# Six stages of attention and expert networks on one core: attention's steps in another order, the sort's one-hot blocks eight at a time, and every semaphore opened at the program's start

## What is computed

```python
x = x + 0.5 * _L0_ffn_ref(_layernorm(x), ...)      # stage 0
x = x + _L0_attn_ref(_layernorm(x), ...)           # stage 1
x = x + 0.5 * _L0_ffn_ref(_layernorm(x), ...)      # stage 2
x = x + 0.5 * _L1_ffn_ref(_layernorm(x), ...)      # stage 3
x = x + _L1_attn_ref(_layernorm(x), ...)           # stage 4
x = x + 0.5 * _L1_ffn_ref(_layernorm(x), ...)      # stage 5

# _L0_attn_ref: patches of 20 tokens at a stride of 2
dots = jnp.einsum('brhsd,brhtd->brhst', q, k) * scale
out = jnp.einsum('brhst,brhtd->brhsd', jax.nn.softmax(dots, axis=-1), v)

# _L1_attn_ref: causal, with a table by clipped distance
scores = (scores + jnp.einsum('bhqd,qkd->bhqk', Qh, rel_k)) / scale
attn = jax.nn.softmax(jnp.where(causal[None, None], scores, -1e9), axis=-1)
out = jnp.einsum('bhqk,bhkd->bhqd', attn, Vh) + jnp.einsum('bhqk,qkd->bhqd', attn, rel_v)

# _L1_ffn_ref: two of eight experts for each token, and a shared one
top_v, top_i = jax.lax.top_k(probs, K)
out_e = jnp.einsum('etf,efd->etd', silu(flat @ w1_e) * (flat @ w3_e), w2_e)
routed = jnp.einsum('te,etd->td', gates, out_e)
return alpha * shared + (1.0 - alpha) * routed
```

## Time and profile before

| | before |
|---|---|
| median of three runs | 1068.61 us (1068.46 to 1072.13) |
| the profiled execution's own time | 1070.65 us |
| span of the profiled execution | 1068.9 us |
| PE busy | 872.8 us (82%) |
| DVE busy | 691.8 us (65%) |
| ACT busy | 458.4 us (43%) |
| POOL busy | 307.1 us (29%) |
| mean granted clock of PE | 0.916 of full speed |

### The profile page before, as it was taken

One profiled execution on the slowest core, in us unless ns is written; L12 is line 12 of the kernel. 1 busy time (PEld: TensorE's weight loads), 2 busy tenths in 40 slices (PEclk: granted clock), 3 DMA queues, 4 the chain that ended last, 5 costly groups with the idle time before them and its releaser, 6 DMA issues.

```text
span 1068.9 us, 21934 instructions
## 1 busy us (share of the span) xinstructions
PE 872.8 (82%) x7943; PEld 684.8 (64%) x7943; DVE 691.8 (65%) x2146; ACT 458.4 (43%) x807; POOL 307.1 (29%) x391
## 2 busy tenths in 40 slices
PE   2899946777769999699999936788887768999996
PEld 1788824444558788588888813445444447988885
DVE  5586556879785877674444458788888558444444
ACT  1333304576744336324554401545455533345542
POOL 5572001001405246205666301000000010266641
PEclk9999965999988999799999956989899868999998
DMA  8800000000000001001111020000000010011113
GB/s 235 260 2 1 1 1 1 2 2 2 2 2 1 2 2 31 11 1 38 42 45 40 16 79 1 2 1 2 2 2 1 2 40 1 15 47 42 46 27 121
DMA packets 27734, 31.26 MB, mean 29 GB/s; under 512 B 5999, under 2 KB 20214, under 8 KB 27632
## 3 DMA queue, kind: packets, MB, share of 16 engines
q1 hardware_dynamic: 22640, 20.55, 6.4%
q0 software_dynamic: 4992, 9.32, 3.3%
HBM read 22.51 MB, written 8.26 MB: 29 GB/s over the span
## 4 chain that ended last, share of the span: by engine, by line
PE 58%; DVE 27%; ACT 9%; issue 3%; DMA 1%; POOL 1%; DVEq 0%; SPq 0%; POOLq 0%; ACTq 0%
PE bank L1397 9%; PE banks0to L1359 5%; PE banks0to L814 5%; DVE score_max L1615 5%; PE banks0to L1360 5%; PE banks0to L1361 5%; PE bank L1383 4%; PE banks0to L822 4%; PE bank L833 3%; PE bank L1886 3%; ACT stacks_and_choice L1798 2%; PE banks0to L1866 2%; DVE expert_sum L563 2%; PE banks0to L1871 2%; ACT hidden L1793 2%
## 5 line engine op out<-in xcount | busy, mean ns | idle before, releaser
L1078 DVE TENSOR_TENSOR hidden<-silu_gate,banks0to 128x512 f32<-128x512 f32 x110 | 75.6, 688 | 146.0 <-PE banks0to L1361 144.5
L1811 ACT ACTIVATE normed_T<-banks0to 128x1024 f32<-128x1024 f32 x80 | 82.5, 1032 | 103.4 <-PE banks0to L1871 103.2
L1291 ACT COPY hidden<-bank 128x512 f32<-128x512 f32 x110 | 64.5, 586 | 132.2 <-PE bank L1383 132.2
L1397 PE MATMUL bank<-l_w,hidden 128*128 (+1 forms) x880 | 117.8, 277 | 2.7 <-ACT hidden L1291 2.7
L1397 PEld LDWEIGHTS bank<-l_w,hidden 128*128 128x128 f32 x880 | 110.2, 193 | 13.3 <-ACT hidden L1291 3.7
L1615 DVE TENSOR_REDUCE score_max<-banks0to 128x8 f32<-128x1024 f32 x80 | 97.6, 1220 | 19.8 <-PE banks0to L1871 17.5
L1256 POOL DMA_INDIRECT stacks_and_choice<-l_ffn_normed,v_tokens x78 | 75.6, 970 | 117.9 <-DVE v_tokens L1243 94.0
L1268 POOL DMA_INDIRECT l_ffn_results<-normed_T,v_tokens x78 | 78.3, 1004 | 73.8 <-DVE normed_T L1099 42.9
L563 DVE SCALAR_TENSOR_TENSOR expert_sum<-bank,gate,expert_sum 128x128 f32<-128x128 f32 x224 | 63.0, 343 | 48.8 <-PE bank L833 47.1
L197 POOL TENSOR_TENSOR ln_rstd<-ln_var_eps,minus_half 128x4 f32<-128x4 f32 x24 | 25.4, 1060 | 236.4 <-DVE ln_var_eps L190 236.4
L1285 ACT ACTIVATE silu_gate<-banks0to 128x512 f32<-128x512 f32 x110 | 65.8, 598 | 44.9 <-PE banks0to L1361 42.9
(11 more groups left out here) (281 smaller groups left out, 1906.0 us busy)
## 6 DMA issues: line engine op xcount, KB each, us to landing
l_w<-in_L_ffn_w_e SPq DMA_DIRECT2D x2, 2048.0 KB, 13.5
stacks_and_choice<-l_ffn_results SPq DMA_DIRECT2D x8, 512.0 KB, 5.6
l_w<-in_L_ffn_w SPq DMA_DIRECT2D x1, 2048.0 KB, 10.1
l_ffn_normed<-stacks_and_choice SPq DMA_DIRECT2D x7, 256.0 KB, 2.3
stacks_and_choice<-l_ffn_normed,v_tokens POOLq DMA_INDIRECT x78, 2.6
l_ffn_results<-normed_T,v_tokens POOLq DMA_INDIRECT x78, 2.3
x_tokens<-in_L_attn_x SPq DMA_DIRECT2D x4, 256.0 KB, 3.7
out_x<-x_tokens SPq DMA_DIRECT2D x4, 256.0 KB, 2.3
```

The source lines that it names most:

```text
L1078: v.tensor_tensor(net.hidden[:, i % 2, :], net.sil[:, i % 2, :], net.bank[2 + i % 2], ALU.mult).then_inc(self.gated.sem, 1)
L1397: ins = mm(net.bank[5 + i % 2][:, 0:D], net.hiddenT[:, i % 2, f, :], w2, start=(f == 0), stop=(f == FT - 1))
L1811: nc.scalar.activation(net.pT[:, i % 2, :, :], net.scores[:, 1], ACT.Exp).then_inc(self.exps.sem, 1)
```

## The change

Nothing that is computed changes, and no instruction goes to another engine. All increments of `prime` move to the start of the program, on each engine. In attention the division of tile 1 moves up to stand right behind that of tile 0; q_stack and k_stack are signalled after each query tile; the first sequence's second projection goes to banks 6 and 7, so that it need not wait until DVE has read banks 4 and 5; and the statistics of groups 1 and 2 stand in front of the reading of the first projection, with group 3 in front of the first maxima. In stage 4 the statistics of group 0 and the first normalisation are done among the last adds of stage 3. In TokenChoice the three operations on one-hot blocks become four times three over eight choices each, one set behind each `at_rows`, and the product of unit 3 moves in front of them; `count` moves on PE behind the next `up`.

```diff
     def token_choice(...):
-        every = [P, T * TOP, BLOCKS]
-        chain.then_wait(v.tensor_tensor(net.which_block, ... .to_broadcast(every), flat(net.choice_block), ALU.is_equal))
-        unit(3)
-        v.tensor_tensor(net.in_block[:, :, 0, :], net.which_block, flat(net.choice_number), ALU.mult)
-        v.tensor_tensor(net.in_block[:, :, 1, :], net.which_block, flat(net.choice_gate),
+        unit(3)
+
+    def in_blocks(self, dve, chain, r):
+        at, every = slice(r * RING, (r + 1) * RING), [P, RING, BLOCKS]
+        chain.then_wait(v.tensor_tensor(net.which_block[:, at, :], ... .to_broadcast(every), flat(net.choice_block), ALU.is_equal))
+        v.tensor_tensor(net.in_block[:, at, 0, :], net.which_block[:, at, :], flat(net.choice_number), ALU.mult)
+        v.tensor_tensor(net.in_block[:, at, 1, :], net.which_block[:, at, :], flat(net.choice_gate),
                         ALU.mult).then_inc(self.placed.sem, 1)
         for r in range(T * TOP // RING):
             at_rows(r)
+            self.in_blocks(dve, chain, r)
...
             step(late + 4 + r)
         def move(c):
-            if c == 0:
-                pe.wait_ge(self.placed.sem, self.placed.at(0, 1))
             if c % RING == 0:
+                pe.wait_ge(self.placed.sem, self.placed.at(0, c // RING + 1))
...
                 up(i + 1)
+            if i == self.late + 1:
+                count()
...
                 turn_hidden(i)
-            if i == self.late:
-                count()
...
         for g in range(groups):
...
+            if attention and g == 1:
+                dve.wait_ge(*self.group_done(0))
+                attention.spread.vector(dve, 0)
+            if attention and g == 2:
+                attention.spread.wait(dve, 0)
+                attention.normalise(dve, 0)
...
 class Attention:
+    def projected(self, n, tt):
+        banks = self.net.bank
+        return banks[6:8] if n == 0 and tt == 1 else banks[4:6]
...
         def split(...):
-            ins.then_inc(self.stacks.sem, 1)
+                ins.then_inc(self.stacks.sem, 1)
         def first():
-            normalise(0)
+            if not self.begun:
+                self.normalise(dve, 0)
...
+            for g in range(1, 3):
+                self.spread.vector(dve, g)
             for tt in range(TPB):
                 project(0, 0, tt, front)
             split(0, 0, front)
...
-            for g in range(1, T // GROUP):
-                self.spread.vector(dve, g)
-            self.spread.wait(dve, T // GROUP - 1)
+            self.spread.vector(dve, T // GROUP - 1)
             project_and_maximise(0, 0)
...
                 finish(n, 0, back)
...
+                finish(n, 1, back)
             project_and_maximise(n + 1, 1 - b, with_max, with_front, then, late)
             if with_max:
                 values(n + 1, 1 - b)
-            finish(n, 1, back)
...
         def stacks(n, b, groups):
             for g in groups:
+                if g % 2 == 0:
+                    pe.wait_ge(self.stacks.sem, self.stacks.at(n, g // 2 + 1))
                 if g == 0:
-                    pe.wait_ge(self.stacks.sem, self.stacks.at(n, 1))
...
         def _(dve):
             for stage in made:
+                stage.prime_vector(dve)
+            for stage in made:
```

127 lines of the change are left out of this document (75 added, 52 removed).

## The result

The changed kernel takes 1061.11 us (median of 11 runs, 1054.1 to 1063.8); the kernel before, beside it, 1068.82 us (11 runs). The ratio is 0.9908 with a 95% interval of 0.9888 to 0.9928: faster by 0.7 to 1.1%. The time lies inside the predicted range (1049.5 to 1063), but the gain is 7.7 us where 12.5 were forecast. The eleven runs lie in two groups, five at 1054.1 to 1058.6 us with a mean granted clock of 0.928 to 0.932 and six at 1061.1 to 1063.8 with 0.915 to 0.918; the profile is of one of the six (1063.62 us), so what it says of lost clock is shown for those alone.

A forecast was written before the change was run, and what follows sets the result against it. PE was busy 82% and DVE 65%, with the bound changing from stage to stage. The terms summed to 12.5 us off the profiled 1070.65, 1058.1; that execution stood 2.0 over the median, so 1056, range 1049.5 to 1063.

The forecast's parts named there:

- The start: Start of the program: DVE's 35 semaphore openings, now all first, delay the first statistic; a loss of 0.4 us.
- the six turns: First attention's turns: early division gains 0.2 us in each of six, the last turn loses; taken as 0 in all.
- The first TokenChoice's start and sort: First TokenChoice up to its first move: start +1.7, count +0.6, shorter block operations; first move 5.2 us sooner.
- The rounds: Three later rounds of each sort, which take over nine block operations: a loss of 0.1 us each.
- The second attention's lead: Second attention up to PE's first stacks: earlier statistics, free banks and half signals gain 6.3 us (4.5 to 6.5).
- The second sort and the clock behind it: Second TokenChoice: the same sort gain, +2.6 us, and +3.4 us from PE's clock no longer halved behind the first move.
- the term of -7.0: Second attention's turns: early division waits 1.2 us for `by_token`, losing 1.0 us seven times; ends -11 and 0.
- the slower rival: PE's clock falls in each turn of both attentions, 2.0 us a turn, giving 1081 us; chance 0.04.
- this rival (gains taken back by row transfers): Gains ahead of TokenChoice's units are taken back by the row fetches, about 1066 us; chance 0.03.
- that the clock held at the second sort: Second TokenChoice's first move: shorter PE wait keeps full clock, +3.4 us; rival that it falls, 1059.5 us, chance 0.15.
- a loss in the first attention's turns: Rival: first attention's `by_token` isn't ready either, so seven turns lose 1.0 us each, 1063 us; chance 0.08.

The follow-up runs named there:

- The taken-back versions: One-hot blocks whole on the changed kernel: 1068.19 us; openings at each stage's head, 1046.36, and count before the `up`, 1049.05, on the kernel with late division and two fillers.
- the runs with one and with three waits filled: Changed kernel plus unread PE transposes in second-attention turns: 16 before the shifted queries, 1060.83 us; also 8 and 14 at two mid-turn waits, 1055.54 us.
- the kernel with the late division and two fillers: Changed kernel with second attention's tile 1 division behind the next maximum again, plus 8 and 14 unread transposes at two mid-turn PE waits: 1046.77 us, ratio to before 0.9800.
- the kernel with three fillers: Changed kernel plus 16, 8 and 14 unread transposes at three PE waits of each second-attention turn: 1055.54 us.

## Why the prediction was right, and where it was short

**Right by its steps.** The start lost 0.4 us (first statistic at 4.14). Up to stage 2's first add 2.3 us were gained (356.17 to 353.89), the forecast for the start and the first attention together: 2.7 by the second sequence's first maximum with the start's loss in it (183.67 to 181.00; 2.3 forecast), 0.4 in each of six turns at full clock (17.4 to 17.0; 0.2 forecast), and the last turn's loss, foreseen at 1.0, of 1.1. The reason given for the six turns was not right: their second divisions wait for nothing without the earlier stacks too. The first TokenChoice's start and sort gave 5.5 for 5.2. The taken-back versions, against the changed kernel's stretch, give 2.9 for the blocks (2.85), 2.0 for the openings (1.7) and 0.6 for the count (0.6), the last two with the clock at half in more of the stretch. The rounds cost 0.12 us each (4.63 in place of 4.51). The second attention's lead gave 6.3 for 6.3. The second sort and the clock behind it gave 5.8 for 6.0.

**The step that costs was named, and its size was not.** The early division waits for `by_token` (1.16 us [<-PE], 1.2 forecast), and a turn without loss of clock is 0.9 us longer (25.9 against 25.0), 1.0 forecast. Mis-sized is the term of -7.0: its price went by turns at full clock, and there it was right, 6.7 us from the stage's first maximum to its end (219.2 against 212.4). In the profile that stretch lost 9.5 us (218.6 to 228.1), within the term's own lower end of -11, and taking the step back alone gave 11.7 in the medians. The difference is clock: the changed kernel's profile lies 9.0 us above the 219.2, the profile before 6.2 above the 212.4. I had it as the slower rival, at 0.04 and against the 2.12 us of wait at 469.70 that did no harm, and that comparison was wrong: one wait that did no harm says nothing of a loop that waits three times in each turn. It did not hold at its own place either: behind the first sort's first move, after 1.55 us of waiting, the clock fell in five of the twelve profiles with the short blocks. The rival in turn was too dear and too wide: 2.0 a turn in both attentions; it was 1.0, in the second. The Trainium skill (TensorE: Matmul & The Clock Gate, A second HAM failure mode: psum-queue depth-cycling) says that short idle times of PE between groups of matmuls, if they are frequent, let its clock swing between the levels; the runs with one and with three waits filled agree, with 26.9 to 27.3 and 25.9 us a turn.

**Missed: what stands behind the stretches that were moved.** Behind stage 2's third add 1.2 us went, where no instruction is moved. This piece takes 28.16 us in three kernels of the study and 29.3 to 30.9 in the others, and the granted clock of its last 20 us is 1.00 in the three and 0.78 to 0.86 in the others. The changed kernel, and the kernel with the late division and two fillers:

```profile
416.40:436.40 20.00, 18.32 (x139) 0.80 0.01 2
```

```profile
410.60:430.60 20.00, 18.55 (x161) 1.00 0.04 14
```

And 2.2 us of the first sort's gain were lost before the rows came back: 0.4 in the rounds, 0.5 by the first routed units, 1.3 in front of the first add, which waits for the transfer of the returned rows. I gave this rival (gains taken back by row transfers) 0.03 and looked for it at the fetch, not at the return. Why the return took longer is not shown; from first move to first add the kernels with the same code spread from 149.8 to 152.4, with 151.2 and more in the five whose clock fell behind the first move.

**Right for a part of its reasons**: that the clock held at the second sort. The wait in front of it was 1.56 us, not the 0.7 to 1.5 expected, and in the profile of the kernel with three fillers the clock did fall in the first rounds of both sorts (half from 463.0 and from 893.1, and a round of 6.2 us in place of 4.6). At the second sort it held in the other eleven profiles with the short blocks.

**Luck.** The sum was 5.4 us too good against the profile: 2.5 in the second attention, 1.9 at the return of the rows and 1.2 at the end of stage 2, with the rest within 0.4. The range held this because its slower end stood for something else, a loss in the first attention's turns, which did not come. The lower five of the eleven runs lie around the forecast of 1056, but no profile of them shows whether they got there by the steps of the sum.

## What to carry to other kernels

Moving a step up to end its engine's work sooner pays only if its input is there: look for the last producer of that input at the new place (here a chain through ACT, 1.2 us later), and count what was filling the wait before. Where PE waits several times in each turn of a loop, cost a longer turn at both clocks, from turns of the trace that had either. And before a few us of a lead are chased, steady the loop behind it, and compare runs at the same mean clock: here a loss of some 3.5 us was hidden in the medians by the clock of the turns.

## What was not expected of the hardware

Work that nobody reads steadied the kernel: with 22 transposes a turn, in waits of 0.83 and 1.07 us, the seven turns took 173.5 to 173.7 us in four of the five profiles that divide late in the second attention with it, and 174.8 in the fifth, against 176.2 and 177.1 in the two without. The shortest runs with the early division were no shorter for it (1054.0 and 1054.1). One wait filled was not enough; the clock then fell at the next ones of the turn. And opening a semaphore is not free on an engine: 13 of them held DVE for some 1.2 us though each record is 21 ns long, and all 35, begun at 0.8 us, ended at 4.0; but what their place was worth in the rows, 2.0 us, was not seen in the time.
